# Gate and up products of the first hidden chunk in two pieces of the rows, for four of eight experts

## The reference, cut to what matters

```
probs = softmax(xt @ router_w + router_b);  rw, ids = top_k(probs, 2)
rw = rw / (sum(rw) + 1e-20)
for e in range(8):
    y = y + w_e * ((silu(xt @ gate_w[e]) * (xt @ up_w[e])) @ down_w[e])
y = y + (silu(xt @ sh_gate_w) * (xt @ sh_up_w)) @ sh_down_w
```

## Time and profile before

| | |
|---|---|
| runs of the kernel | 345.56, 340.32, 344.79 us; median 344.79 |
| the profiled execution | 344.11 us, its span 342.3 us |
| granted TensorE clock, mean over the span | 0.99 |
| busy: PE / PEld / DVE / ACT / POOL | 323.1 / 270.2 / 221.3 / 173.2 / 148.3 us |
| HBM | 107 GB/s over the span |

### The profile page before, as it was taken

One profiled execution on the slowest core, in us unless ns is written; L12 is line 12 of the kernel. 1 busy time (PEld: TensorE's weight loads), 2 busy tenths in 40 slices (PEclk: granted clock), 3 DMA queues, 4 the chain that ended last, 5 costly groups with the idle time before them and its releaser, 6 DMA issues.

```text
span 342.3 us, 8467 instructions
## 1 busy us (share of the span) xinstructions
PE 323.1 (94%) x3508; PEld 270.2 (79%) x3508; DVE 221.3 (65%) x577; ACT 173.2 (51%) x370; POOL 148.3 (43%) x167
## 2 busy tenths in 40 slices
PE   7999899998879989999999999997989899898996
PEld 5785578876479989999999999997557686676864
DVE  1099798997887444556555554556955788666774
ACT  0304674557233255766676666533038870586700
POOL 5201019900607847888798889864600001000020
PEclk9999999999989999999999999998999999999999
DMA  7991003320022173575766764165000000000002
GB/s 261 404 394 62 3 0 98 88 87 3 0 95 83 58 232 105 188 232 189 228 202 199 223 182 161 45 204 213 1 0 2 2 4 3 0 1 4 4 2 71
DMA packets 16016, 37.09 MB, mean 108 GB/s; under 512 B 1930, under 2 KB 9729, under 8 KB 15976
## 3 DMA queue, kind: packets, MB, share of 16 engines
q1 hardware_dynamic: 14576, 33.68, 29.6%
q0 software_dynamic: 960, 2.43, 2.3%
q10 hardware_dynamic: 440, 0.41, 0.5%
HBM read 30.76 MB, written 5.75 MB: 107 GB/s over the span
## 4 chain that ended last, share of the span: by engine, by line
PE 63%; DVE 18%; ACT 6%; POOL 5%; issue 4%; DMA 3%; POOLq 0%; ACTq 0%; SPq 0%; DVEq 0%
PE ps L1551 10%; PE ps L1552 9%; PE ps L1553 9%; PE ps L1749 5%; PE ps L1338 3%; POOL xg_d L1296 3%; PE ps L1759 3%; PE ps L1845 2%; PE ps L1821 2%; PE ps L1350 2%; DMA xgs<-xg_d 2%; ACT stage_l L475 1%; DVE stage_l L840 1%; PE ps L1882 1%; DVE mx L834 1%
## 5 line engine op out<-in xcount | busy, mean ns | idle before, releaser
L1253 POOL TENSOR_TENSOR w0l<-raw,w0h 128x384 fp32r<-128x384 f32 (+1 forms) x60 | 56.3, 972 | 13.0 <-ACT w0h L541 12.7
L1269 POOL TENSOR_TENSOR rstd<-vtmp,cst 128x3 f32<-128x3 f32 (+1 forms) x8 | 6.7, 838 | 111.0 <-DVE vtmp L739 58.7
L1030 DVE TENSOR_TENSOR ps<-gact,ps 128x256 f32<-128x256 f32 (+3 forms) x60 | 26.3, 438 | 35.7 <-ACT gact L565 34.8
L1253 POOL TENSOR_TENSOR w1l<-raw,w1h 128x384 fp32r<-128x384 f32 (+1 forms) x48 | 44.8, 974 | 6.7 <-ACT w1h L541 5.8
L565 ACT ACTIVATE gact<-ps 128x256 f32<-128x256 f32 (+3 forms) x60 | 23.2, 387 | 19.9 <-PE ps L1553 19.4
L569 ACT ACTIVATE hrh<-ps 128x256 fp32r<-128x256 f32 (+1 forms) x48 | 18.4, 383 | 28.0 <-DVE ps L1030 28.0
L1035 DVE TENSOR_TENSOR hrl<-ps,hrh 128x256 fp32r<-128x256 f32 (+1 forms) x48 | 20.4, 424 | 18.4 <-ACT hrh L569 18.4
L1338 PE MATMUL ps<-cst 128*128 128x512 f32 x62 | 27.9, 595 | 0.0
L1551 PE MATMUL ps<-xg0h,w1h 128*128 128x256 f32 x88 | 25.8, 293 | 0.0
L1551 PE MATMUL ps<-xg1h,w0h 128*128 128x256 f32 x88 | 25.7, 292 | 0.0
L1552 PE MATMUL ps<-xg1l,w0h 128*128 128x256 f32 x88 | 24.9, 283 | 0.0
(11 more groups left out here) (301 smaller groups left out, 926.1 us busy)
## 6 DMA issues: line engine op xcount, KB each, us to landing
raw<-in_wexp SPq DMA_DIRECT2D x18, 768.0 KB, 4.4
raw<-in_wexp SPq DMA_DIRECT2D x9, 640.0 KB, 4.7
xg_d<-zero SPq DMA_DIRECT2D x8, 256.0 KB, 10.7
xgs<-xg_d SPq DMA_DIRECT2D x8, 256.0 KB, 5.0
stage_l<-in_xT SPq DMA_DIRECT2D x6, 320.0 KB, 5.1
yg_d<-y SPq DMA_DIRECT2D x7, 256.0 KB, 4.1
stage_l<-in_tokW SPq DMA_DIRECT2D x6, 128.0 KB, 5.2
wq_l<-in_wql SPq DMA_DIRECT2D x1, 640.0 KB, 5.3
```

What stands on the lines that cost most here:

```text
L1030: V.tensor_tensor(up, gact[i % 2][rows_of(c), 0:n], up, ALU.mult).then_inc(S("hm"), 1)
L1253: last = nc.gpsimd.tensor_tensor(wset[i][1][w], raw[w], wset[i][0][w].bitcast(F32), ALU.subtract)
```

## The change

For chunk 0 of experts 0 to 3, `gate_up` goes through the moving rows in two pieces, each with both feature blocks and the three matmuls of `split3`; the pieces are 128 and 128 columns for experts 0 and 1, and 192 and 64 for experts 2 and 3. All other calls have one piece of 256, as before. The waits ahead and the signal behind stay where they are.

```diff
+            def pieces_of(e, c):
+                if c > 0 or e >= 4:
+                    return [(0, CAP)]
+                edge = CAP // 2 if e < 2 else 3 * CAP // 4
+                return [(0, edge), (edge, CAP)]
+
             def gate_up(e, c):
 ...
                 for part in parts_of(c):
-                    for k in range(DC):
-                        last = split3(bank(4 + g % 3)[:, part * CAP:(part + 1) * CAP],
-                                      gate_up_chunk(wset[(e + 1) % 2], part, k, c),
-                                      [x[:, k, :] for x in xg[e % 2]], k == 0, k == DC - 1, True)
+                    for lo, hi in pieces_of(e, c):
+                        for k in range(DC):
+                            last = split3(bank(4 + g % 3)[:, part * CAP + lo:part * CAP + hi],
+                                          gate_up_chunk(wset[(e + 1) % 2], part, k, c),
+                                          [x[:, k, lo:hi] for x in xg[e % 2]], k == 0, k == DC - 1, True)
                 last.then_inc(S("gu"), 1)
```

## The result

The changed kernel takes 350.92 us (median of 4 runs, 347.93 to 355.01), the kernel before 345.18 us in the same session. The ratio is 1.021, with a 95% interval of 1.0135 to 1.0285. Two later sessions give 1.017 (1.0143 to 1.0197) and 1.0243 (1.0181 to 1.0304). The changed kernel is slower in all three; whether by more than 2% they leave open. The medians count every execution of a session, the ratios leave out those in a slower state of the chip. The forecast was 350.0 us in a range of 346 to 362.

The account below looks back on a forecast made before the run. TensorE was taken to bound the experts' stage: four calls at +1.35 us give +5.4, less 0.18 covered, so +5.2 us; on the median of 344.79 that gives 350.0 us, range 346 to 362.

Parts of the forecast that it names:

- The bound: Experts' stage: TensorE busy throughout turns of 13.03 us, so each nanosecond added there adds a nanosecond to the time.
- The price: Chunk 0, experts 0 to 3: 24 load-bound narrow matmuls at 0.116 us replace 12 at 0.119; +1.35 us a call.
- The cover: Expert 0, behind its twelve matmuls: longer pieces cover TensorE's 0.18 us wait for VectorE's split of the shared expert.
- Other engines at nothing: Experts' turns: work on ScalarE, POOL and SyncE's queue moves with TensorE and costs nothing; POOL gets more room.
- More instructions at nothing: Whole program: fetching 96 more instructions costs nothing, since 8-column matmuls are issued every 0.111 us.
- Rival 1: Pieces under 256 columns: narrow fp32r runs as plain fp32 does; +15.1 to +18.7 us, 360 to 363.5 us; chance 0.26.
- Rival 2: Narrow pieces: columns alone decide, the load hides; -0.4 to +0.8 us, about 345 us; chance 0.08.
- The skill's 81 ns: Narrow matmuls: a documented 81 ns per load and matmul pair at 128 columns would give +2.1 us in all.
- Rival 3: Something hidden behind TensorE comes forward or the clock differs; one to two us, either way; chance 0.02 as main thing.

Follow-up runs that it names:

- first profile: Profiled execution of the changed kernel itself, no further edit, the longest of its runs: 355.01 us.
- second profile: Another profile of the same changed kernel, without a low clock in the experts' stage: 351.81 us.
- first repeat: The changed kernel, unedited, timed again in more rounds against the kernel before: 349.95 against 343.58 us, ratio 1.017.

## Why the prediction was right

- **The bound.** TensorE is busy in every turn before and after, and splitting every product adds 53.4 us for 528 matmuls, with TensorE busy for whole turns. Right. (From 95 to 237 us PE waits five times and not three: for the selection, 1.0 us, and behind the loop for ScalarE, 0.7, as well. Neither lies in a turn of the earlier trace rows.)
- **The price.** Foreseen 0.111 to 0.119 us a narrow matmul, taken 0.116; measured 0.111 to 0.112 for 8, 64, 128 and 192 columns, 0.114 for 248. The 0.012 us by which an fp32r stream of 256 exceeds its columns doesn't come on top of a load-bound one, so the lower end, straight from the 8-column rows, would have been the better choice: +1.24 us a call and not +1.35.
- **The cover.** 0.18 us of expert 0's wait foreseen; the stretch is 1.14 longer and not 1.24, so 0.1 was given back: the rest of the 0.18 was the distance that a 64-row product has anyway, not a wait. The 0.15 us in the turn of the bf16 transposes was missed. Sum in the stage: 5.2 foreseen, 4.7 measured.
- **Other engines at nothing.** Right, by the turns' rows.
- **More instructions at nothing.** Wrong, and the one failed step: 1.4 to 2.1 us of stalls far behind the change. They made up for the price and the cover taken 0.5 us too high.
- **The number.** The mechanism and the 4.7 us are shown; that 350.92 lies so close to 350.0 is partly luck. By ratio the three sessions give +7.2, +5.8 and +8.3 us where +5.2 was forecast, so the difference was put too low each time, by 0.6 to 3 us; of that the stalls, less the 0.5 us above, explain 1.2.
- **Rival 1** (four passes) is out: no distance grows with the width, one row to a product. **Rival 2** is out for four-byte operands and true for bf16 ones: its 0.055 us came from bf16 rows, and the runs give 0.057.
- **The skill's 81 ns** (the section "Back-to-back issue gap", cited above): neither form shows it here. A pair with 128 columns is 0.111 us in fp32r and 0.057 us in bf16.
- **Rival 3**, the clock: it explains part of the first profile's 355.01 us, in which the stretch of expert 0 with 6.83 us at the low level took 14.13 us against 11.51 in the second profile. It doesn't explain the first repeat, where the changed kernel's granted clock was no lower (mean 0.992) than that of the kernel before (0.989).

## What to carry to other kernels

Ask what a matmul's load costs before narrowing what streams past it: here, with 128x128 four-byte weights, every piece of 8 to 248 columns costs 0.111 to 0.114 us, against 0.120 for 256, so a cut of the moving side nearly doubles the price, while with bf16 weights the cut in half is free. A load of 64 stationary columns halves the price of a narrow piece (0.060 us), but twice as many are needed. The rows for it were in the trace before, in unrelated products of 8 columns with the same load. And a control that has the instructions but not the work tells the cost of a change from the cost of a longer program.

## What the runs showed that I had not expected

- The clock fell from 2.4 to 1.2 GHz with each of four rows of 48 matmuls of 64 columns, three times within the row and once 1 us behind it, with no gap in TensorE's records in the row, and raised the distance to 0.213 us. With 24 in a row and wide ones between, it didn't fall in the turns. The Trainium skill, "TensorE: Matmul & The Clock Gate", section "HAM oscillation", advises against idle gaps; here there was none to be seen, so a busy row alone is no guard.
- 96 more instructions bring a stall of "issue", about 0.6 us, into each of two fast rows of small matmuls over 100 us behind the change; of three kernels with 288 more, one has such a stall and two have none.
- Behind the first narrow matmul after wide ones the next starts after 0.05 us (64 columns), and behind the first wide one after narrow ones only after 0.18; together they come to the same as two equal distances of 0.112. Why was not tried.
